# Half of the last chunk's experts weighed behind the output projection on ScalarE, and summed on VectorE over a turned view

## What is computed

```python
def moe_proj(p):
    y = jnp.einsum('nc,ech->neh', x, p)
    return jnp.einsum('ne,neh->nh', w, y)
q, k, v = (moe_proj(p).reshape(b, t, -1) for p in (q_proj, k_proj, v_proj))
scores = jnp.einsum('bth,bsh->bts', q, k) / sqrt(128)
attn = softmax(scores)
o = jnp.einsum('bts,bsh->bth', attn, v).reshape(n, h)
z = jnp.einsum('ne,nh->enh', w, o)
out = jnp.einsum('enh,ehc->nc', z, o_proj)
```

## Time and profile before

| | before |
|---|---|
| median of 3 executions | 490.58 us (490.44 to 490.92) |
| profiled execution, own time | 490.49 us |
| its span, first to last instruction | 488.7 us |
| TensorE busy | 438.8 us (90%) |
| VectorE busy | 410.8 us (84%) |
| ScalarE busy | 244.6 us (50%) |
| GpSimd busy | 62.7 us (13%) |
| mean granted TensorE clock | 0.965 |

### The profile page before, as it was taken

One profiled execution on the slowest core, in us unless ns is written; L12 is line 12 of the kernel. 1 busy time (PEld: TensorE's weight loads), 2 busy tenths in 40 slices (PEclk: granted clock), 3 DMA queues, 4 the chain that ended last, 5 costly groups with the idle time before them and its releaser, 6 DMA issues.

```text
span 488.7 us, 9719 instructions
## 1 busy us (share of the span) xinstructions
PE 438.8 (90%) x3791; PEld 304.3 (62%) x3791; DVE 410.8 (84%) x919; ACT 244.6 (50%) x446; POOL 62.7 (13%) x77
## 2 busy tenths in 40 slices
PE   8999999998899989401899899999999999999997
PEld 6447999987358754100279876667656666655676
DVE  6997889777797659999876689986998999989786
ACT  5976555473856629895655554336224222423110
POOL 0007000000590705500081000000000000000000
PEclk9999999999999999855999998999999999999999
DMA  8979997950560003403330016545863000000000
GB/s 271 352 303 392 386 382 301 372 240 23 150 173 1 1 0 129 130 0 129 130 98 1 1 43 221 170 178 180 280 237 97 7 12 7 5 7 7 6 7 28
DMA packets 24629, 66.71 MB, mean 137 GB/s; under 512 B 3108, under 2 KB 6567, under 8 KB 24455
## 3 DMA queue, kind: packets, MB, share of 16 engines
q1 hardware_dynamic: 24144, 65.98, 37.7%
q10 hardware_dynamic: 438, 0.11, 0.1%
HBM read 38.68 MB, written 1.18 MB: 82 GB/s over the span
## 4 chain that ended last, share of the span: by engine, by line
PE 25%; DVE 25%; issue 4%; ACT 1%; DVEq 0%
PE bk L758 8%; DVE XT L1741 6%; DVE X L1729 4%; PE bk L766 4%; DVE RA L1769 4%; PE bk L803 3%; PE bk L625 2%; DVE RA L1548 1%; DVE WK L1590 1%; PE bk L778 1%; PE bk L634 1%; PE bk L668 1%; PE bk L685 1%; DVE QS L1456 1%; PE bk L694 1%
## 5 line engine op out<-in xcount | busy, mean ns | idle before, releaser
L758 PE MATMUL bk<-X,RB 128*128 128x512 f16 x384 | 94.6, 383 | 0.6 <-DVE X L1729 0.4
L1061 ACT ACTIVATE X<-RA 128x512 f16<-128x512 f32 x64 | 40.3, 630 | 100.9 <-DVE RA L1769 84.7
L1741 DVE SCALAR_TENSOR_TENSOR XT<-bk,WK,XT 128x128 f32<-128x128 f32 x192 | 67.0, 349 | 5.4 <-issue 0.2
L758 PEld LDWEIGHTS bk<-X,RB 128*128 128x128 f16 x384 | 37.0, 98 | 42.3 <-DVE X L1729 1.6
L766 PEld LDWEIGHTS bk<-RB,X 128*128 128x128 f16 x768 | 48.4, 98 | 15.4 <-issue 0.6
L766 PE MATMUL bk<-RB,X 128*128 128x128 f16 x768 | 53.5, 220 | 0.0
L1729 DVE TENSOR_TENSOR X<-RA,X 128x512 f16<-128x512 f32 x64 | 43.9, 685 | 1.1 <-ACT X L1061 1.1
L899 ACT ACTIVATE WK<-bk 128x512 f32<-128x512 f32 x48 | 28.6, 595 | 27.5 <-PE bk L414 21.9
L803 PE MATMUL bk<-RB,RA 128*128 128x512 f16 x144 | 38.8, 379 | 0.9 <-DVE RA L1786 0.9
L1357 DVE SCALAR_TENSOR_TENSOR RB<-WK,WCOL,bk 128x512 f32<-128x512 f32 x32 | 23.7, 744 | 10.0 <-ACT WK L899 10.0
L414 PE MATMUL bk<-X,RC 128*128 128x128 f16 x480 | 29.7, 219 | 0.0
(11 more groups left out here) (345 smaller groups left out, 887.3 us busy)
## 6 DMA issues: line engine op xcount, KB each, us to landing
RC<-RA SPq DMA_DIRECT2D x20, 768.0 KB, 5.2
STG<-RA SPq DMA_DIRECT2D x8, 768.0 KB, 5.3
RC<-expert_weights SPq DMA_DIRECT2D x22, 256.0 KB, 6.2
RC<-in_wx SPq DMA_DIRECT2D x7, 768.0 KB, 8.2
X<-in_w SPq DMA_DIRECT2D x8, 512.0 KB, 3.5
RA<-RA SPq DMA_DIRECT2D x4, 768.0 KB, 5.0
STG<-expert_weights SPq DMA_DIRECT2D x12, 256.0 KB, 6.5
QT<-expert_weights SPq DMA_DIRECT2D x8, 256.0 KB, 4.6
```

The costliest lines, as they stand in the source:

```text
L758: t = e.matmul(BK[m][:, :], P16[:, wp, wo:wo + 128], ZH[:, n % 4, xp, :], start=(e1 == 0 and i == 0), stop=(e1 == 15 and i == 2))
L1061: e.activation(ZH[:, r, 0, :], zf[r], ACT.Copy).then_inc(S("z_hi"), 1)
L1741: stt(XT[:, bb_(t_)], bank_o(n)[:, bb_(i)], RW[:, t_, e1:e1 + 1], XT[:, bb_(t_)], ALU.mult, ALU.add).then_inc(S("acc"), 1)
```

## The change

Four things change in the end of the kernel.

1. For chunk 3 only experts 0 to 7 (`PRE = 8`) are still weighed ahead of the product. Experts 8 to 15 go the way of the other chunks: eight more groups (numbers 48 to 55: tile b, g = 2 and 3) are added to `groups`. They need chunk 3's result in 16-bit halves, which VectorE makes in `last_halves` behind ZW 1, and its `RW` divided by the softmax's sum, one more multiply behind `inverse_sum(3)`.
2. The groups from `LATE = 44` on (tile 11 and the eight new ones) are weighed by ScalarE: `late(n)` makes four 128x128 copies with a pointer scale from PSUM to a buffer in SBUF. The first stands between `softmax(3)` and `ptt(3)`, the other eleven behind it.
3. VectorE sums the weighed pieces with one reduction for each tile (`sum_up`) over the view "p (e n) -> p n e": 16 experts for tile 11 (2048 elements), 8 for each tile of chunk 3 (1024 elements), and adds the result to `XT`.
4. TensorE's list is new: behind each of the experts 0 to 7 come one or two output groups, and expert 7 gives the `tile` signals.

```diff
+        PRE, LATE = 8, 44
+        groups += [(3, b, g) for b in range(4) for g in range(PRE // 4, 4)]
+        GRP = (16 - PRE) // 4
+        WGT = [XF[:, 512 * i:512 * i + 512] for i in range(4)] + [big(i // 4)[:, 512 * (i % 4):512 * (i % 4) + 512] for i in range(4 * GRP)]
+        SUM = PTT[:, 0:640].rearrange("p (b n) -> p b n", b=5)
...
             def output(n):
                 c, b, g = groups[n]
                 q.wait_ge("ot_lo", c + 1)
-                q.wait_ge(*(("acc", 4 * (n - 2)) if n >= 3 else ("wts", 3)))
+                q.wait_ge(*(("late_w", n - 2 - LATE) if n - 3 >= LATE else ("acc", 4 * (n - 2)) if n >= 3 else ("wts", 3)))
...
-                t.then_inc(S("prod_o"), 1)
+                t.then_inc(S("prod_o" if n < LATE else "late"), 1)
...
-                return e.matmul(BK_T[b][:, 0:128], ZW[e1][:, bb_(b)], WO[:, bb_(e1)], start=(e1 == 0), stop=(e1 == 15), skip_group_check=True)
-
-            for e1 in range(12):
+                return e.matmul(BK_T[b][:, 0:128], ZW[e1][:, bb_(b)], WO[:, bb_(e1)], start=(e1 == 0), stop=(e1 == PRE - 1), skip_group_check=True)
+
+            n = 46
+            for e1 in range(PRE):
                 for b in range(4):
-                    weighed_output(e1, b)
-                if e1 in (0, 4):
-                    output(46 + (e1 == 4))
-            for b in range(4):
-                for e1 in range(12, 16):
                     t = weighed_output(e1, b)
-                t.then_inc(S("tile"), 1)
+                    if e1 == PRE - 1:
+                        t.then_inc(S("tile"), 1)
+                for _ in range(1 if e1 < 3 else 2):
+                    if n < len(groups):
+                        output(n)
+                        n += 1
...
+            def late(n):
+                c, b, g = groups[n]
+                t_ = 4 * c + b
+                q.wait_ge("late", n - LATE + 1)
+                q.wait_ge("rw", c + 1)
+                if n == LATE:
+                    q.wait_ge("qkvmm", 12)
+                if n == LATE + 4:
+                    q.wait_ge("otmm", 4)
+                for i in range(4):
+                    e1 = 4 * g + i
+                    t = e.activation(WGT[n - LATE][:, bb_(i)], bank_o(n)[:, bb_(i)], ACT.Copy, scale=RW[:, t_, e1:e1 + 1])
+                t.then_inc(S("late_w"), 1)
+
             softmax(3)
+            late(44)
             ptt(3)
+            for n in range(45, len(groups)):
+                late(n)
...
             inverse_sum(3)
-            for e1 in range(16):
+            q.wait_ge("rs", 4)
+            tt(RW[:, 12:16, :], RW[:, 12:16, :], RS[:, 12:16].unsqueeze(2).to_broadcast([128, 4, 16]), ALU.mult).then_inc(S("rw"), 1)
+
+            def sum_up(i):
+
+                t_, first, many = (11, 0, 4) if i == 0 else (11 + i, 4 + GRP * (i - 1), GRP)
+                q.wait_ge("late_w", first + many)
+                q.wait_ge("otmm", 4)
+                src = XF[:, 0:2048] if i == 0 else RA[:, 512 * (first - 4):512 * (first - 4 + many)]
+                red(SUM[:, i, :], src.rearrange("p (e n) -> p n e", n=128), X_AX, ALU.add).then_inc(S("sum"), 1)
+                q.wait_ge("sum", i + 1)
+                q.wait_ge("turned", 4)
+                tt(XT[:, bb_(t_)], XT[:, bb_(t_)], SUM[:, i, :], ALU.add).then_inc(S("summed"), 1)
+
+            def last_halves():
+                e.tensor_copy(OT16[:, 0, cc(3)], BK[4][:, :]).then_inc(S("ot_hi3"), 1)
+                q.wait_ge("ot_hi3", 1)
+                tt(OT16[:, 1, cc(3)], BK[4][:, :], OT16[:, 0, cc(3)], ALU.subtract).then_inc(S("ot_lo"), 1)
+
+            for e1 in range(PRE):
                 q.wait_ge("otmm", 4)
                 q.wait_ge("zlo", NI)
                 q.wait_ge("qkvmm", 12)
                 tt(ZW[e1], BK[4][:, :], WR[16 + e1], ALU.mult).then_inc(S("zw"), 1)
-                if e1 in (1, 4, 7, 10):
-                    gather({1: 44, 4: 45, 7: 46, 10: 47}[e1])
+                if e1 == 1:
+                    last_halves()
+            sum_up(0)
             for b in range(4):
                 t_ = 12 + b
+                sum_up(b + 1)
                 q.wait_ge("tile", b + 1)
                 q.wait_ge("rs", 4)
-                q.wait_ge("turned", 4)
+                q.wait_ge("summed", b + 2)
                 stt(XT[:, bb_(t_)], BK_T[b][:, 0:128], RS[:, t_:t_ + 1], XT[:, bb_(t_)], ALU.mult, ALU.add).then_inc(S("done"), 1)
```

More of the change, by code:

```diff
@@ L51 @@
      ("ffmm", 24), ("ffdown", 12), ("x3mm", 4), ("mlp_up", 16), ("prod_q", 60)),
-    (("down", 48), ("weffmm", 4), ("ret_amm", 1), ("fwt", 3), ("wbotmm", 8), ("zmm", 4), ("mlp_down", 16), ("prod_o", 48), ("tile", 4)),
+    (("down", 48), ("weffmm", 4), ("ret_amm", 1), ("fwt", 3), ("wbotmm", 8), ("zmm", 4), ("mlp_down", 16), ("prod_o", 44), ("late", 12), ("tile", 4)),
     (("mean", 4), ("vvmm", 4), ("turn0", 1), ("turnw0", 1), ("qkvmm", 12)),
@@ L64 @@
     (("gated", 48), ("weff", 4), ("sin", 32), ("fw_lo", 3), ("k", 4), ("g", 8), ("x1", 4), ("l_max", 4), ("l_lo", 4),
-     ("ff_max", 24), ("gate16", 4), ("gated_ff", 5), ("ot_ff", 4), ("o_lo", 12), ("x2", 4), ("pp", 4), ("w2", 2), ("weighed", 64), ("zw", 16)),
+     ("ff_max", 24), ("gate16", 4), ("gated_ff", 5), ("ot_ff", 4), ("o_lo", 12), ("x2", 4), ("pp", 4), ("w2", 2), ("weighed", 64), ("zw", 8)),
     (("xg", 4), ("kadd", 4), ("l_hi", 4), ("gated16_0", 1), ("o_max", 4), ("o_hi", 12), ("x4", 4), ("zlo", 64)),
@@ L69 @@
     (("const", 2), ("sh_lo", 2), ("sim_sq", 1), ("ffs", 4), ("k_out", 4)),
-    (("x_lo", 4), ("xq", 4), ("quant", 12), ("ot_lo", 3)),
-    (("route", 30), ("router", 114), ("rw", 3), ("done", 4)),
+    (("x_lo", 4), ("xq", 4), ("quant", 12), ("ot_lo", 4)),
+    (("route", 30), ("router", 114), ("rw", 4), ("done", 4)),
     (("chosen", 5), ("l1p", 1), ("relm", 1), ("cos", 32), ("p16", 8)),
@@ L834, in weighed_output @@
                     q.wait_ge(*(("qv_out", 8), ("k_out", 4), ("qv_out", 8), ("ptt", 4))[b])
-                return e.matmul(BK_T[b][:, 0:128], ZW[e1][:, bb_(b)], WO[:, bb_(e1)], start=(e1 == 0), stop=(e1 == 15), skip_group_check=True)
-            for e1 in range(12):
+                return e.matmul(BK_T[b][:, 0:128], ZW[e1][:, bb_(b)], WO[:, bb_(e1)], start=(e1 == 0), stop=(e1 == PRE - 1), skip_group_check=True)
+            n = 46
+            for e1 in range(PRE):
                 for b in range(4):
-                    weighed_output(e1, b)
-                if e1 in (0, 4):
-                    output(46 + (e1 == 4))
-            for b in range(4):
-                for e1 in range(12, 16):
-                    t = weighed_output(e1, b)
-                t.then_inc(S("tile"), 1)
+                    t = weighed_output(e1, b)
+                    if e1 == PRE - 1:
[4 more added lines that the diff above has]
+                        n += 1
+            while n < len(groups):
+                output(n)
+                n += 1
         def scalar(e):
@@ L1981, in sync @@
                     t_ = 4 * c + b
-                    q.wait_ge(*(("acc", 4 * groups.index((c, b, 3)) + 4) if c < 3 else ("done", b + 1)))
+                    q.wait_ge(*(("done", b + 1) if c == 3 else ("summed", 1) if t_ == 11 else ("acc", 4 * groups.index((c, b, 3)) + 4)))
                     e.dma_start(out[bb_(t_), :], XT[:, bb_(t_)]).then_inc(S(f"out{c}"), 16)
```

## The result

The changed kernel takes 494.36 us (median of five executions, 493.72 to 498.55) against 490.58: 1.0087 times the time before, with a 95% interval of 1.0048 to 1.0125. Run again later beside the kernel before it took 494.68 us against 490.87, 1.0079 (1.0063 to 1.0094). It is slower, by some 3.8 us where 1.7 were forecast.

A forecast was written before the change was run, and what follows sets the result against it. VectorE was taken to set the end up to 483.04, then TensorE's products and one VectorE sum. Start +0.5, tile 0 -1.6, stretch behind it 5.87 - 3.03 gave +1.7: 490.49 to 492.2 us, range 491.3 to 494.9.

The forecast's parts named there:

- The sign and its mechanism: VectorE waits for tile 0 before tile 1's sum, idle 4 us, three sums follow; slower, chance 0.82 in all.
- the dense price: VectorE's reductions over the turned view cost as dense ones: 1.22 us for 1024 elements, 2.29 for 2048.
- rival (a): VectorE's turned view is slow: three sums on the path at 1.99 us, time 494.5; chance 0.25.
- The second prop: TensorE's reads 64 bytes apart at 0.89 ns each are quicker than VectorE's 1.04; another engine's port, decides nothing.
- The start: Four weighings on ScalarE ahead of the attention copy delay L835's first product by 0.5 us, to 468.96.
- Tile 0: TensorE's first tile signal comes at 482.5 us, after 7.25 experts and all ten output groups.
- After the tile: VectorE's first tile sum, then three rounds of reduction, addition and tile sum at 1.84 us: 5.87 us against 3.03 before.
- The end behind the last sum: The last output transfer still follows VectorE's last sum by 2.05 us.
- Rival (b): ScalarE becomes the bound if its evictions do not overlap: +0.3 us, or about 494.6 at 0.45 each; chance 0.07.
- Rival (c): TensorE's ten groups cost under 0.65 us each, so tile 0 comes earlier; 489.7 at 0.40; chance 0.10.

The follow-up runs named there:

- sums_first: The changed kernel with all five turned sums of VectorE ahead of the four tile sums that wait for tiles; 492.93 us, ratio 1.0048.
- strides: The changed kernel plus twelve VectorE operations behind its last sum (eight reductions at strides 4 to 512 bytes, four multiplications); 511.19 us, only these operations' durations read.
- ptt_first: The changed kernel with ScalarE's copy of the turned attention, ptt(3), ahead of the first group of weighings, late(44); 494.22 us, ratio 1.0084.
- combo: The changed kernel with pieces written turned by ScalarE and read densely, all sums ahead of the tile waits, and ptt(3) ahead of late(44); 490.24 us, ratio 0.9991.
- earlier: The kernel with those three repairs together, and TensorE's output groups placed one expert earlier; 489.31 us, ratio 0.9971.
- turned_writes: The changed kernel with ScalarE writing its weighed pieces in turned order, so that VectorE's reductions read densely; 492.60 us, ratio 1.0042.
- dense_view: The changed kernel with the five reductions read over a dense view instead of the turned one (sums of other elements); 492.01 us, ratio 1.0035.

## Why the prediction was right or wrong

**The sign and its mechanism were right.** The kernel is slower because VectorE waits for tile 0 ahead of sums that do not need it, so that three of them follow the tile. `sums_first` changes only this and wins 2.3 us of the stretch. The dense kernel that the forecast had in mind has a stretch 1.61 us over before, where the forecast said 1.7.

**The step that failed** is "I take the dense price all the same, because L1444 does two such accesses for each element and the reduction one". The term was 3 x 1.22 us on the path and measured 3 x 1.87, 1.95 us more; `strides` shows that one scattered stream costs as much as two (1.01 us each, 0.69 dense). The dense and the scattered price both stood in the prediction, and it chose the wrong one: rival (a), with a chance of 0.25, a price of 1.99 us and a time of 494.5, is what happened. The range up to 494.9 holds the measured time only because it took in that rival. That 494.5 is so near is partly luck: the three sums were 3 x 0.12 us shorter than at L1444's price and tile 0 came 0.3 earlier, against 0.2 of waits that the forecast had not counted and 0.2 by which the medians differ more than the stretches. The second prop, TensorE's strided reads at 0.89 ns for a column, was said to decide nothing and decided nothing. Two figures do not come out of their rows. 465.44 + 1.02 is 466.46 and not 466.37 for the copy, so by its own terms the late start was 0.6 us, where 0.5 was put and 0.49 came. L1444's 0.99 us for 512 elements is 1.93 ns for each and not 1.83, on which nothing hangs.

**Term by term.** The start: +0.5 forecast, 8.80 - 8.31 = 0.49 measured, and `ptt_first` gives it back. Tile 0: forecast at 482.5, which is 22.4 us after the q eviction; measured 22.04. An expert behind a group costs 0.89 us in the chain of waits (the row at 471.38), not 0.95, eight records of 0.111 instead of 0.119; a group costs 0.65 as forecast. After the tile: forecast 5.87 us, measured 490.84 - 482.81 = 8.03. Of the 2.16 us between them 1.95 are the stride, and 3 x 0.07 the wait between the addition and the tile sum, 0.10 us where I had put 0.03. The end behind the last sum: 2.05 forecast, 2.06 measured. Together +0.49 - 1.92 + 5.00 = +3.57 us for the stretch (tile 0 without the late start 1.92 us earlier than at 23.47, and 8.03 against 3.03 behind it), which is the time that the medians show within 0.3.

**Rival (b)**, ScalarE as the bound, did not come: its groups took 1.03 to 1.1 us and TensorE never waited for one. (In `combo` and `earlier` ScalarE did become the bound, by what VectorE waits for and not through TensorE.) **Rival (c)** needed tile 0 more than 1.7 us earlier than forecast and got 0.3.

**What was not seen** is that VectorE's last sums also set the pace of SP's transfers. In the changed kernel it did not matter, since they came 2.57 us apart.

## What to carry to other kernels

Before a sum over a turned view goes on the path, look for any row in the trace of the same engine with a stride of 16 bytes or more and take its price, without splitting it among its streams. If the writer can turn the data at no loss of pace, let it. In an engine's in-order list put what waits for nothing ahead of what waits: here the same work lost 3.8 us or won 2.7 by order and layout. Work moved to an idle engine can still cost: ask what stands behind it in that engine's list (here the copy, 0.5 us) and when its results are needed.

## What the runs showed of the hardware that was not expected

- On VectorE one scattered stream costs the same as two, at the one stride measured for this, 64 bytes: 1.01 us for a 128x512 multiplication with the read, the write or both turned, against 0.69 dense (`strides`).
- The step lies between 8 bytes (1.22 us for a reduction of 1024 elements) and 16 (1.96); 64 to 512 bytes are slightly cheaper (1.87; `strides`).
- ScalarE's evictions with results 32 bytes apart last 0.49 us instead of 0.38, but four in a row follow one another at the same 0.257 us (`turned_writes`, `dense_view`).
- Four output transfers of 64 KB issued in a row on SP start 0.38, 0.47 and 0.48 us apart, and all but the first take 0.43 us to issue where one alone takes 0.33; when their data come faster than that, the last one is late (`earlier`: 0.58 us).
